# A four-layer scan and attention kernel: three layer scans as one unrolled stream, with layers 1 and 2 at 18 and 36 steps behind layer 0

## The chip, the cores and the metric

The kernel runs on one core of a Trainium2 chip. The time is device microseconds (us) of one execution. TensorE is the matrix engine, VectorE, ScalarE and GpSimd do the elementwise work, and SyncE issues most of the transfers. The profile calls them PE (PEld for its weight loads), DVE, ACT, POOL and SP; a "q" behind a name is that engine's instruction queue.

## The reference, cut to what matters

`x` has shape (batch 8, time 512, features 512), all in fp32. Three recurrent layers run over time, each with a residual, and then one causal attention layer with 16 heads.

```
# layer 0, a gated cell
fused  = sigmoid([x_t, h] @ w_W + w_b)               # (8, 1024)
reset, keep = split(fused, 2)
memory = x_t @ wx_W + wx_b + reset * (h @ wh_W + wh_b)
h      = keep * h + (1 - keep) * tanh(memory)
x = x + all h
# layers 1 and 2, each
h = tanh(x_t @ Wx + b + h @ Wh);   x = x + all h
# layer 3
x = x + attention(x)
```

Step t of a layer needs its own step t-1 and the x of step t that the layer before has left. The products with x_t don't depend on h, so they can be made for many steps at a time.

## The kernel before, in words

**Layout.** All of x stays on chip, transposed, in the tile `X` (feature on 128 partitions, 4 feature groups, batch 8, time 512), so 16 steps of it are (batch, time) with time innermost. `setup` (L398) loads 32 tiles of 128 rows through four buffers `xrows`, turns each with four TensorE transposes (L470) into one of two banks and copies it to `X`, the even ones on VectorE (L508) and the odd ones on ScalarE (L438). ScalarE's queue issues the loads of layer 0's weights, recurrent and input parts by turns. Then GpSimd copies the first 16 steps of `X` into `stage` (L453), and TensorE makes layer 0's 12 groups of products for them (L480).

**Fills.** Time is cut into 32 chunks of 16 steps, so a chunk is 128 columns (16 steps x 8 batches). A *fill* is one group of 128 output features of x @ Wx for one chunk: 16 matmuls in four groups of columns (L225), which VectorE adds a bias to and keeps in `xw0` or `xw12` (L290). Layer 0 has 12 fills a chunk, layers 1 and 2 have 4 each. The matmuls read a chunk from `stage[layer]`, where it lies as (time, batch), contiguous. GpSimd copies it there out of `X` (L381), after VectorE has added the states of the layer before to `X` (L309).

**Steps.** Step n of the stream does on TensorE, in this order: layer 0's products with its state, first those for reset and memory (L181), then those for keep (L187); one product for layers 1 and 2 together (L201); the fills planned for this step (L225). VectorE does in step n: for layers 1 and 2 of step n-1 a transpose out of the bank (L269) and an addition of the input part (L272); it keeps the fills of step n-1 (L290); it does the chunk additions planned here (L309); and then comes layer 0's chain: transpose (L328), addition (L330), transpose and addition for keep (L335, L337), L342 and L345 for the memory, L348, and after ScalarE's tanh L351 and L356, which writes the new state. ScalarE does the tanh of layers 1 and 2 of step n-1 (L237), two sigmoids (L250, L253) and a tanh (L256).

**Rounds and blocks.** A round m is 16 steps; `plan(m)` (L62) says what it holds. Layer 0 runs in rounds 0 to 31 on chunk m, layer 1 in rounds 2 to 33 on chunk m-2, layer 2 in rounds 4 to 35 on chunk m-4, so they are 32 and 64 steps behind. A round's fills are spread evenly over its steps. Four rounds are a block with instruction streams of its own: blocks 0, 4, 28 and 32 are written out, and the five between are a hardware loop over one block. After each block all engines meet and the semaphores are cleared (`clear_signals`, L89), with 9 blocks in all. The last block also loads the attention's weights (L168). A small block adds layer 2's last chunk to `X` on GpSimd (L394). Then come the attention's setup and the attention, which the change leaves alone.

**What sets the order.** Every engine runs its instructions in the written order and waits on counting semaphores.

Of the kernel before, what the change touches and what calls it, by code (L numbers as in the profile page):

```python
# [31 lines left out]
ROUNDS = NCH + 4  # L32
# [3 lines left out]
PER_BLOCK = 4  # L36
RAMP = 8
# [12 lines left out]
def fills_of(m):  # L50

    out = []
    if -1 <= m < NCH - 1:
        out += [(0, g) for g in range(G0)]
    if 0 <= m - 1 < NCH:
        out += [(1, g) for g in range(KC)]
    if 0 <= m - 3 < NCH:
        out += [(2, g) for g in range(KC)]
    return out

def plan(m):  # L62

    fills = fills_of(m)
    n = len(fills)

    late = 0 if m < NCH - 1 else 3
    by_step = [[]] * late + [fills[n * s // (CH - late):n * (s + 1) // (CH - late)] for s in range(CH - late)]
    chunk_ops = [[] for _ in range(CH)]  # L70
    if m < NCH - 1:
        chunk_ops[0].append(("stage", 0, m + 1))
    at = 1
    for layer, c in ((1, m - 1), (2, m - 3)):
        if 0 <= c < NCH:
            chunk_ops[at].append(("add", layer - 1, c))
            chunk_ops[at + 1].append(("stage", layer, c))
        at += 2
    if 0 <= m - 5 < NCH:
        chunk_ops[at].append(("add", 2, m - 5))  # L80
    layers = [l for l, c in ((0, m - 2), (1, m - 4)) if 0 <= c < NCH]
    return {"scan0": 0 <= m < NCH, "scan12": layers, "fills": by_step, "chunk_ops": chunk_ops}
# [17 lines left out]
def scan_rounds(nc, mem, sems, a, first, times):  # L100

    plans = [plan(first + u) for u in range(PER_BLOCK)]
    steps = [(u, t) for u in range(PER_BLOCK) for t in range(CH)]
    S = len(steps)
    if times > 1:
        with nc.Fori(0, times) as i:
            scan_block(nc, mem, sems, a, plans, steps, S, first, i)
            clear_signals(nc, mem)
    else:
        scan_block(nc, mem, sems, a, plans, steps, S, first, None)  # L110
        clear_signals(nc, mem)

def scan_block(nc, mem, sems, a, plans, steps, S, first, i):
    s = sems
    X, stage, h0, h12, xw0, xw12 = mem.X, mem.stage, mem.h0, mem.h12, mem.xw0, mem.xw12

    def counts(per_step):  # L120
        out = [0]
        for u, t in steps:
            out.append(out[-1] + per_step(u, t))
        return out

    n0 = counts(lambda u, t: int(plans[u]["scan0"]))
    n12 = counts(lambda u, t: int(bool(plans[u]["scan12"])))
    nfill = counts(lambda u, t: len(plans[u]["fills"][t]))
    nchunk = counts(lambda u, t: len(plans[u]["chunk_ops"][t]))

    staged = {}

    q = 0
    for u, t in steps:
        for kind, layer, c in plans[u]["chunk_ops"][t]:
            q += 1
            if kind == "stage":
                staged[u, layer] = q
    last_fill = {}
    q = 0  # L140
    for u, t in steps:
        for layer, g in plans[u]["fills"][t]:
            q += 1
            last_fill[u, layer] = q

    def before(u, t):

        return (u % 2, t - 1) if t else (1 - u % 2, CH - 1)

    with nc.Block(no_gpsimd_drain=True) as block:  # L150

        if first == 0:
            @block.sync
            def _(sp):

                for l in (1, 2):
                    for dst, src in ((mem.wx[l], a[f"L{l}_Wx"]), (mem.wh12[:, l - 1, :, :], a[f"L{l}_Wh"])):
                        sp.dma_start(dst[:, :, :], src.rearrange("(k p) n -> p k n", p=P)).then_inc(s.weights_in, 16)
                sp.wait_ge(s.weights_in, 64)

        if first >= NCH:
            @block.sync
            def _(sp):

                loads = [(mem.uk_rows, a["uk_w"]), (mem.uv_rows, a["uv_w"]), (mem.w_proj, a["proj_w"]),
                         (mem.w_qkv, a["qkv_w"])]
                for dst, src in loads:
                    sp.dma_start(dst[:, :, :], src.rearrange("(k p) n -> p k n", p=P)).then_inc(s.weights_in, 16)  # L168
                sp.wait_ge(s.weights_in, 16 * len(loads))

        @block.tensor
        def _(pe):
            def main0(n, u, t):

                if n0[n]:
                    pe.wait_ge(s.h0_new, n0[n])
                us, ts = before(u, t)
                for k in range(KC):
                    for j in range(KC):  # L180
                        mm = pe.matmul(mem.ps0[32 * j:32 * j + B, 0:2 * P],  # L181
                                       h0[:, us, k, ts, :], columns_of(mem.wh0[:, k, 0:3:2, :], j),
                                       start=(k == 0), stop=(k == KC - 1))
                mm.then_inc(s.reset_done, 1)
                for k in range(KC):
                    for j in range(KC):
                        mm = pe.matmul(mem.ps0o[32 * j:32 * j + B, 0:P],  # L187
                                       h0[:, us, k, ts, :], columns_of(mem.wh0[:, k, 1:2, :], j),
                                       start=(k == 0), stop=(k == KC - 1))
                mm.then_inc(s.update_done, 1)  # L190

            def main12(n, u, t):

                if n12[n]:
                    pe.wait_ge(s.h12_new, n12[n])
                us, ts = before(u, t)
                ls = plans[u]["scan12"]
                l0, l1 = ls[0], ls[-1] + 1
                for k in range(KC):
                    for j in range(KC):  # L200
                        mm = pe.matmul(mem.ps12[32 * j:32 * j + B * len(ls), P * l0:P * l1],  # L201
                                       h12[:, us, k, ts, l0:l1, :].rearrange("p l b -> p (l b)"),
# [4 lines left out]
            for n, (u, t) in enumerate(steps):  # L207
                p = plans[u]
                if p["scan0"]:
                    main0(n, u, t)  # L210
                if p["scan12"]:
                    main12(n, u, t)

                if n >= 2 and p["fills"][t] and nfill[n - 1]:
                    pe.wait_ge(s.fill_kept, nfill[n - 1])
                for f, (layer, g) in enumerate(p["fills"][t]):
                    pe.wait_ge(s.chunk_op, staged[u, layer])
                    if first == 0 and layer:
                        pe.wait_ge(s.weights_in, 64)  # L220
                    w = mem.wx[layer]
                    for k in range(KC):
                        for j in range(KC):
                            at = g * P + 32 * j
                            mm = pe.matmul(mem.fillps[n % 2][32 * j:32 * (j + 1), f * N:(f + 1) * N],  # L225
                                           w[:, k, at:at + 32], stage[layer][:, k, :],
                                           start=(k == 0), stop=(k == KC - 1))
                    mm.then_inc(s.fill_done, 1)

        @block.scalar  # L230
        def _(act):
            def tanh12(n, u, t):
                act.wait_ge(s.pre12, n12[n] + 1)

                ls = plans[u]["scan12"]
                l0, l1 = ls[0], ls[-1] + 1
                nc.scalar.activation(h12[:, u % 2, :, t, l0:l1, :].rearrange("p k l b -> p l k b"), mem.sum12[:, l0:l1, :, :],  # L237
                                     ACT.Tanh).then_inc(s.h12_new, 1)

            for n, (u, t) in enumerate(steps):  # L240
                p = plans[u]
                if n:
                    v, w = steps[n - 1]
                    if plans[v]["scan12"]:
                        tanh12(n - 1, v, w)
                if n and t == 0 and p["scan12"] and nchunk[n]:
                    act.wait_ge(s.chunk_op, nchunk[n])
                if p["scan0"]:
                    act.wait_ge(s.pre0, n0[n] + 1)
                    nc.scalar.activation(mem.gates0[:, 0:KC, :], mem.pre0[:, 0:KC, :],  # L250
                                         ACT.Sigmoid).then_inc(s.gates0, 1)
                    act.wait_ge(s.pre0o, n0[n] + 1)
                    nc.scalar.activation(mem.gates0[:, KC:2 * KC, :], mem.pre0[:, KC:2 * KC, :],  # L253
                                         ACT.Sigmoid).then_inc(s.update0, 1)
                    act.wait_ge(s.memory0, n0[n] + 1)
                    nc.scalar.activation(mem.tanh0[:, :, :], mem.mem0[:, :, :],  # L256
                                         ACT.Tanh).then_inc(s.tanh0, 1)
            u, t = steps[-1]
            if plans[u]["scan12"]:
                tanh12(S - 1, u, t)  # L260

        @block.vector
        def _(dve):
            def pre12(n, u, t):

                ls = plans[u]["scan12"]
# [5 lines left out]
                nc.vector.tensor_tensor(  # L272
                    mem.sum12[:, l0:l1, :, :],
                    mem.tp12[:, 0:2 * apart].rearrange("p (l x) -> p l x", l=2)[:, l0:l1, 0:P]
                    .rearrange("p l (q c) -> p l q c", q=KC)[:, :, :, 0:B],
                    xw12[:, u % 2, l0:l1, :, t, :], ALU.add).then_inc(s.pre12, 1)

            def keep_fills(n, u, t):

# [1002 lines left out]
```

## Time and profile before

| | us |
|---|---|
| median of 3 runs | 4083.1 (4080.97 to 4084.29) |
| the profiled execution | 4085.57 |
| its span, first to last instruction | 4083.9 |
| TensorE busy in it | 3902.9 |
| VectorE busy in it | 2336.8 |

The granted TensorE clock has a mean of 0.983 of full speed. Matmuls overlap each other, so their busy time is more than the distance of their starts; for a sum it is the starts that count. A matmul in fp32 is two records, so a group of 16 matmuls stands as x32.

### The profile page before, as it was taken

Reading aid. Unit: us, or ns where it says so; the run is one execution under the profiler, and the core shown is the slowest. Engines: PE = TensorE matmul, PEld = TensorE weight load, DVE = VectorE, ACT = ScalarE, POOL = GpSimd, SP = SyncE. Lnnn points to the kernel's source line nnn. Section 1 sums busy time; section 2 is a strip of 40 time slices with the busy share of each in tenths; the row PEclk is TensorE's granted clock in tenths of the full one; section 3 lists DMA queues with packets and bytes.
Section 4 is the critical chain, followed back from the end, with each engine's and each line's share of the span. In section 5 each row is a group of like instructions: output and inputs, shape, how many; then the busy total and the mean of one; then the engine's idle time right before and its main releaser. Section 6 shows DMA issues by size and latency. Waiting matters only on the chain. (4 is left out here: it accounts for less than half of the span.)

```text
span 4083.9 us, 170825 instructions
## 1 busy us (share of the span) xinstructions
PE 3902.9 (96%) x77684; PEld 2648.1 (65%) x77684; DVE 2336.8 (57%) x8378; ACT 1064.0 (26%) x3931; POOL 158.9 (4%) x373
## 2 busy tenths in 40 slices
PE   6799999999999999999999999998679999999998
PEld 4577777777666666678887777765435555555555
DVE  3565655666566566556556655665326656666564
ACT  1111111111111111111111111111005555555554
POOL 0000000000000000000000000000000000000000
PEclk9999999999999999999999999999969999999999
DMA  5000000000000000000000000001000000000000
GB/s 187 3 4 4 3 3 3 3 4 3 3 3 3 4 3 3 3 4 3 3 4 3 3 3 3 3 3 64 2 6 1 14 11 9 11 12 14 11 6 19
DMA packets 34256, 46.75 MB, mean 11 GB/s; under 512 B 5820, under 2 KB 22252, under 8 KB 33527
## 3 DMA queue, kind: packets, MB, share of 16 engines
q1 hardware_dynamic: 31222, 29.43, 2.3%
q8 instruction: 617, 10.11, 1.0%
q10 hardware_dynamic: 2304, 6.29, 0.4%
q14 instruction: 113, 0.92, 0.1%
HBM read 27.33 MB, written 8.39 MB: 9 GB/s over the span
## 5 line engine op out<-in xcount | busy, mean ns | idle before, releaser
L201 PE MATMUL bank<-wh,h 128*16 128x256 f32 (+1 forms) x17408 | 1002.7, 370 | 52.6 <-ACT h L237 50.8
L181 PE MATMUL bank<-wh,h 128*8 128x256 f32 x16384 | 991.0, 381 | 62.2 <-DVE h L356 31.3
L201 PEld LDWEIGHTS bank<-wh,h 128*16 128x16 f32 (+1 forms) x17408 | 540.1, 97 | 333.9 <-ACT h L237 75.6
L181 PEld LDWEIGHTS bank<-wh,h 128*8 128x8 f32 x16384 | 482.4, 90 | 379.0 <-DVE h L356 50.2
L328 DVE STREAM_TRANSPOSE tp<-bank 128x256 f32<-128x256 f32 x512 | 230.4, 450 | 644.1 <-PE bank L181 644.1
L187 PE MATMUL bank<-wh,h 128*8 128x128 f32 x16384 | 550.9, 274 | 0.0
L187 PEld LDWEIGHTS bank<-wh,h 128*8 128x8 f32 x16384 | 455.6, 90 | 106.2 <-issue 2.5
L250 ACT ACTIVATE gates_sb<-pre_sb 128x32 f32<-128x32 f32 x512 | 117.5, 230 | 1357.6 <-DVE pre_sb L330 1357.6
L225 PE MATMUL bank<-stage,w_qkv 128*32 128x128 f32 x11904 | 386.4, 273 | 0.0
L225 PEld LDWEIGHTS bank<-stage,w_qkv 128*32 128x32 f32 x11904 | 344.3, 110 | 42.6
L237 ACT ACTIVATE h<-sum 128x64 f32<-128x64 f32 (+1 forms) x544 | 137.8, 253 | 786.9 <-DVE sum L272 786.9
L269 DVE STREAM_TRANSPOSE tp<-bank 128x256 f32<-128x256 f32 (+1 forms) x544 | 236.1, 434 | 179.7 <-PE bank L201 118.0
L290 DVE TENSOR_SCALAR xw<-bank,biasT 128x128 f32<-128x128 f32 x628 | 209.6, 349 | 172.3 <-PE bank L225 172.3
L857 ACT ACTIVATE probs<-probs,neg_max 128x385 f32<-128x385 f32 (+3 forms) x512 | 280.2, 554 | 0.0
L870 ACT COPY probsT<-bank 128x512 f32<-128x512 f32 x320 | 174.9, 587 | 369.0 <-PE bank L784 369.0
L946 DVE CUSTOM_DVE_ANT_0 probs<-bank,addends 128x384 f32<-128x384 f32 (+3 forms) x512 | 219.8, 486 | 82.7 <-PE bank L760 80.3
L225 PE MATMUL bank<-stage,wx 128*32 128x128 f32 x8192 | 262.4, 273 | 0.0
L225 PEld LDWEIGHTS bank<-stage,wx 128*32 128x32 f32 x8192 | 235.9, 110 | 29.3
L737 PE MATMUL bank<-X,w_qkv 128*128 128x512 f32 x512 | 236.3, 605 | 9.1 <-PEq L91 5.9
L381 POOL COPY stage<-X 128x512 f32 (+1 forms) x95 | 108.8, 1145 | 2764.6 <-DVE X L309 1387.0
L335 DVE STREAM_TRANSPOSE tp<-bank 128x128 f32<-128x128 f32 x512 | 162.2, 317 | 81.9 <-PE bank L187 77.0
L784 PE MATMUL bank<-ident,probs 128*128 128x128 f32 x1280 | 184.0, 283 | 5.3 <-ACT probs L857 5.0
(131 smaller groups left out, 3346.8 us busy)
## 6 DMA issues: line engine op xcount, KB each, us to landing
xrows<-in_x_dram SPq DMA_DIRECT2D x32, 256.0 KB, 3.8
out_dram<-X SPq DMA_DIRECT2D x32, 256.0 KB, 2.6
w_qkv<-in_L_cond_c_attn_w_dram SPq DMA_DIRECT2D x1, 3072.0 KB, 17.7
wh<-in_L_cond_w_W_dram ACTq DMA_DIRECT2D x4, 512.0 KB, 8.5
w_qkv<-in_L_cond_w_W_dram ACTq DMA_DIRECT2D x4, 512.0 KB, 10.3
wx<-in_L_cond_Wx_dram SPq DMA_DIRECT2D x2, 1024.0 KB, 8.3
wh<-in_L_cond_Wh_dram SPq DMA_DIRECT2D x2, 1024.0 KB, 10.5
mask_all<-in_mask_Bx1x1xS_ff_dram SPq DMA_DIRECT2D x8, 256.0 KB, 3.3
```

Source lines behind the costliest of these rows:

```text
L181: mm = pe.matmul(mem.ps0[32 * j:32 * j + B, 0:2 * P], h0[:, us, k, ts, :], columns_of(mem.wh0[:, k, 0:3:2, :], j), start=(k == 0), stop=(k ...
L187: mm = pe.matmul(mem.ps0o[32 * j:32 * j + B, 0:P], h0[:, us, k, ts, :], columns_of(mem.wh0[:, k, 1:2, :], j), start=(k == 0), stop=(k == K ...
L201: mm = pe.matmul(mem.ps12[32 * j:32 * j + B * len(ls), P * l0:P * l1], h12[:, us, k, ts, l0:l1, :].rearrange("p l b -> p (l b)"), columns_ ...
L225: mm = pe.matmul(mem.fillps[n % 2][32 * j:32 * (j + 1), f * N:(f + 1) * N], w[:, k, at:at + 32], stage[layer][:, k, :], start=(k == 0), st ...
L269: nc.vector.transpose(mem.tp12[:, P * l0:P * l1], mem.ps12[:, P * l0:P * l1]).then_inc(s.turned12, 1)
L290: nc.vector.tensor_scalar(dst, mem.fillps[n % 2][:, f * N:(f + 1) * N].rearrange("p (t b) -> p t b", b=B), mem.biasT[:, bias:bias + 1], No ...
L328: nc.vector.transpose(mem.tp0[:, 0:2 * P], mem.ps0[:, 0:2 * P]).then_inc(s.turned0, 1)
L737: mm = pe.matmul(bank[:, :], mem.w_qkv[:, k, at:at + P], mem.X[:, k, u, :], start=(k == 0), stop=(k == KC - 1))
L784: mm = pe.transpose(bank[:, x * P:(x + 1) * P], mem.probs[qc][:, g, 1 + k * P:1 + (k + 1) * P], mem.ident[:, :])
L857: nc.scalar.activation(row, row, ACT.Exp, bias=mem.neg_max[:, slot, g:g + 1], scale=-1.0, accum_out=mem.sums[:, slot, g:g + 1]).then_inc(s ...
L870: nc.scalar.copy(mem.probsT[v % 2][:, HPG * r * P:HPG * (r + 1) * P], bank[:, :]).then_inc(s.turn_kept, 1)
L946: nc.vector.tensor_tensor_reduce(out=mem.probs[qc][:, g, 1:1 + n], in0=mem.banks[g][:, 0:n], in1=mem.addends[:, TRI[qc]:TRI[qc] + n], scal ...
```

## The change

- All 548 steps (512 of layer 0, and 36 more) are one block, unrolled, with no loop and no meeting of the engines in it. Layer 1 runs 18 steps behind layer 0, layer 2 36 behind.
- Layers 1 and 2 keep their states in a ring of 32 steps. Their places in it and in `xw12` now differ by 2, so VectorE adds the input part for each of the two layers by an instruction of its own.
- The fills have fixed places. In a round of 16 steps, steps 0 and 1 hold two fills of layer 1 each, steps 2 and 3 two of layer 2, and steps 4 to 15 one of layer 0.
- A chunk sum on VectorE (steps 0, 2 and 4) writes x plus the states to `stage`, in (time, batch), for layers 1 and 2; the sum behind layer 2 goes to `X`. A sum whose states wrap around the ring is two instructions. GpSimd has no part in it. `stage` has two slots for each of the two layers.
- Layer 0's fills read the chunk from `X` itself, with batch innermost at a distance of 512 elements.
- Setup loads and turns only 8 of the 32 x tiles (time 0 to 127 of every batch). The other 24 are loaded by SyncE during the scan, turned by TensorE at the end of steps 2 to 25, and copied by ScalarE one step later. The input weights are issued ahead of the recurrent ones. Weights of layers 1 and 2 are loaded between x tiles.
- The weights of the attention are issued when layer 0's last product is done. The last chunk's addition is on VectorE, in the same block.

```diff
-ROUNDS = NCH + 4
-PER_BLOCK = 4
-RAMP = 8
+LAG12 = [CH + 2, 2 * (CH + 2)]
+STEPS = T + LAG12[1]
+HR = 2 * CH
+XR = 4
+TILES = [(b, tc) for tc in range(T // P) for b in range(B)]
+EARLY = B
+TILE_STEP = 2
...
+def fills_of(n):
+
+    m, t = divmod(n, CH)
+    if t < 2 and 0 <= m - 1 < NCH:
+        return [(1, m - 1, 2 * t + g) for g in range(2)]
+    if 2 <= t < 4 and 0 <= m - 2 < NCH:
+        return [(2, m - 2, 2 * (t - 2) + g) for g in range(2)]
+    if t >= 4 and m + 1 < NCH:
+        return [(0, m + 1, t - 4)]
+    return []
+
+
+def sum_of(n):
+
+    m, t = divmod(n, CH)
+    layer = {0: 0, 2: 1, 4: 2}.get(t)
+    if layer is not None and 0 <= m - 1 - layer < NCH:
+        return layer, m - 1 - layer
+    return None
...
+            for i in range(len(tiles)):
+                load_tile(i)
+                if i == XR - 1:
+                    load_layer(1)
+                if i == 2 * XR - 1:
+                    load_layer(2)
...
+                        rows = stage[layer - 1][:, c % 2, k, :] if layer else x_chunk(c)[:, k].rearrange("p b t -> p t b")
...
+            def turn_tile(i):
+                pe.wait_ge(s.x_in[i % XR], 16 * (i // XR + 1))
+                if i >= 2:
+                    pe.wait_ge(s.x_kept, i - 1)
+                for k in range(KC):
+                    mm = pe.transpose(mem.xps[i % 2][:, k * P:(k + 1) * P],
+                                      mem.xrows[:, i % XR, k * P:(k + 1) * P], mem.ident[:, :])
+                mm.then_inc(s.x_turned, 1)
+
+            for n in range(STEPS):
+                if n < T:
+                    main0(n)
+                if layers_of(n):
+                    main12(n)
+                if fills_of(n):
+                    fills(n)
+                if tile_of(n) is not None:
+                    turn_tile(tile_of(n))
...
+            for n in range(STEPS + 1):
+                if n and layers_of(n - 1):
+                    tanh12(n - 1)
+                if n and tile_of(n - 1) is not None:
+                    i = tile_of(n - 1)
+                    b, tc = tiles[i]
+                    act.wait_ge(s.x_turned, i + 1)
+                    nc.scalar.copy(X[:, :, b, tc * P:(tc + 1) * P],
+                                   mem.xps[i % 2][:, :].rearrange("p (k t) -> p k t", k=KC)).then_inc(s.x_kept, 1)
+                if n < T:
+                    gates(n)
...
+                for l in ls:
+                    ins = nc.vector.tensor_tensor(mem.sum12[:, l, :, :], turned[:, l, :, 0:B],
+                                                  xw12[:, l, at[l] // CH % 2, :, at[l] % CH, :], ALU.add)
+                ins.then_inc(s.pre12, 1)
...
+            def chunk_sum(layer, c):
+                if layer:
+                    first = c * CH + LAG12[layer - 1]
+                    dve.wait_ge(s.h12_new, n12[first + CH])
+                    dve.wait_ge(s.chunk_sum, summed[layer - 1, c])
...
+                    if layer < 2:
+                        dst = stage[layer][:, c % 2, :, :].rearrange("p k (t b) -> p k t b", b=B)[:, :, rows, :]
+                        old = before[:, :, rows, :] if layer else in_x.rearrange("p k b t -> p k t b")
+                        ins = nc.vector.tensor_tensor(dst, old, states, ALU.add)
+                    else:
+                        ins = nc.vector.tensor_tensor(in_x, before[:, :, rows, :].rearrange("p k t b -> p k b t"),
+                                                      states.rearrange("p k t b -> p k b t"), ALU.add)
+                ins.then_inc(s.chunk_sum, 1)
...
-            pool.wait_ge(s.x_kept0, len(tiles) // 2)
-            pool.wait_ge(s.x_kept1, len(tiles) // 2)
-            nc.gpsimd.tensor_copy(mem.stage[0][:, :, :].rearrange("p k (t b) -> p k b t", b=B),
-                                  mem.X[:, :, :, 0:CH]).then_inc(s.chunk_op, 1)
...
-            m = 0
-            while m < ROUNDS:
-                times = (NCH - 1 - m) // PER_BLOCK if m == RAMP else 1
-                scan_rounds(nc, mem, sems, a, m, times)
-                m += PER_BLOCK * times
-            add_last_chunk(nc, mem)
+            scan(nc, mem, sems, a)
             clear_signals(nc, mem)
```

## Rows read from the trace of the kernel before

**Rows 1.** The page, part 1: busy us, share of the span and count by engine.

```profile
PE 3902.9 (96%) x77684; PEld 2648.1 (65%) x77684; DVE 2336.8 (57%) x8378; ACT 1064.0 (26%) x3931; POOL 158.9 (4%) x373
```

**Rows 2.** The timeline, all layers: start us, us, engine, line, operation, idle before, releaser.

```profile
1503.07 1.90 PE L181 MATMUL bank<-wh,h 128*8 128x256 f32 x32
1503.32 0.35 DVE L290 TENSOR_SCALAR xw<-bank,biasT 128x128 f32<-128x128 f32 x1 [0.17 <-PE bank L225]
...
1505.05 0.45 DVE L328 STREAM_TRANSPOSE tp<-bank 128x256 f32<-128x256 f32 x1 [1.38 <-PE bank L181]
...
1505.67 1.90 PE L201 MATMUL bank<-wh,h 128*16 128x256 f32 x32
...
1507.32 0.19 DVE L356 TENSOR_TENSOR h<-held,fresh_sb 128x32 f32<-128x32 f32 x1
...
1507.40 1.92 PE L225 MATMUL bank<-stage,wx 128*32 128x128 f32 x64
...
1509.14 1.90 PE L181 MATMUL bank<-wh,h 128*8 128x256 f32 x32
1509.40 0.61 DVE L290 TENSOR_SCALAR xw<-bank,biasT 128x128 f32<-128x128 f32 x2 [1.04 <-PE bank L225]
```

**Rows 3.** The timeline, layer 0 alone: two successive steps.

```profile
75.79 1.91 PE L181 MATMUL bank<-wh,h 128*8 128x256 f32 x32 [0.83 <-DVE h L356]
...
80.28 1.91 PE L181 MATMUL bank<-wh,h 128*8 128x256 f32 x32 [0.83 <-DVE h L356]
```

**Rows 4.** The timeline of TensorE: first instruction of three blocks.

```profile
360.91 1.91 PE L181 MATMUL bank<-wh,h 128*8 128x256 f32 x32 [2.27 <-PEq L91]
...
1064.69 3.60 PE L181 MATMUL bank<-wh,h 128*8 128x256 f32 x32 [5.87 <-issue]
...
2481.33 1.91 PE L181 MATMUL bank<-wh,h 128*8 128x256 f32 x32 [2.08 <-PEq L91]
```

**Rows 5.** The timeline in setup: three turned tiles, the first fills, the scan's first step.

```profile
43.60 2.05 PE L470 MATMUL bank<-ident,xrows 128*128 128x128 f32 x12 [0.39 <-DMA xrows<-in_x_dram]
...
52.67 12.61 PE L480 MATMUL bank<-stage,w_qkv 128*128 128x128 f32 x96 [1.97 <-issue]
...
66.81 1.91 PE L181 MATMUL bank<-wh,h 128*8 128x256 f32 x32 [1.54 <-PEq L91]
```

**Rows 6.** The timeline of the run-out: pairs of successive steps, and the last addition.

```profile
2820.70 1.92 PE L201 MATMUL bank<-wh,h 128*16 128x256 f32 x32 [1.57 <-PEq L91]
2823.73 1.92 PE L201 MATMUL bank<-wh,h 128*16 128x256 f32 x32 [1.11 <-ACT h L237]
...
2920.25 1.06 PE L201 MATMUL bank<-wh,h 128*8 128x128 f32 x32 [1.06 <-ACT h L237]
2922.24 1.06 PE L201 MATMUL bank<-wh,h 128*8 128x128 f32 x32 [0.93 <-ACT h L237]
...
2956.99 1.89 PE L201 MATMUL bank<-wh,h 128*8 128x128 f32 x32 [0.93 <-ACT h L237]
2959.81 1.89 PE L201 MATMUL bank<-wh,h 128*8 128x128 f32 x32 [0.93 <-ACT h L237]
...
2994.78 1.46 POOL L394 TENSOR_TENSOR X<-X,h 128x512 f32<-128x512 f32 x1 [68.77 <-DVEq L389]
```

**Rows 7.** Two stretches: length, busy us (count) by engine, clock, DMA share, GB/s.

```profile
10.00:20.00 10.00, 6.41 (x25) 4.26 (x25) 3.58 (x16) 2.45 (x3) 0.00 (x0) 1.00 1.04 412
...
2953.50:2993.60 40.10, 26.51 (x448) 14.85 (x448) 8.36 (x31) 3.44 (x15) 0.00 (x0) 0.51 0.01 2
```

**Rows 8.** Groups of instructions on VectorE, 300 to 2818: busy, mean ns, idle.

```profile
L272 DVE TENSOR_TENSOR sum<-tp,xw 128x64 f32<-128x64 f32 x447 | 100.7, 225 | 15.4
...
L309 DVE TENSOR_TENSOR X<-X,h 128x512 f32 x60 | 63.3, 1056 | 0.0
...
L272 DVE TENSOR_TENSOR sum<-tp,xw 128x32 f32<-128x32 f32 x13 | 2.5, 193 | 0.4
```

**Rows 9.** The page, part 6: issue of an x tile, KB, us to landing.

```profile
xrows<-in_x_dram SPq DMA_DIRECT2D x32, 256.0 KB, 3.8
```

More of the change, by code:

```diff
@@ L47, with layers_of, counts, ring_parts @@
 NBIAS = _at
[L50 to L58, printed above, removed]
-    return out
[L62 to L82, printed above, removed]
+def layers_of(n):
+    return [l for l in range(2) if 0 <= n - LAG12[l] < T]
+def fills_of(n):
[13 more added lines that the diff above has]
+    return None
+def counts(per_step):
+    out = [0]
+    for n in range(STEPS + 1):
+        out.append(out[-1] + per_step(n))
+    return out
+def ring_parts(first):
+    slot = first % HR
+    head = min(CH, HR - slot)
+    return [(0, slot, head)] + ([(head, 0, CH - head)] if head < CH else [])
 class Mem:
@@ L97, in columns_of @@
     return rows.rearrange("p g (q j r) -> p j g q r", q=KC, j=KC)[:, j]
[L100 to L111, printed above, removed]
@@ L114, in scan_block @@
-def scan_block(nc, mem, sems, a, plans, steps, S, first, i):
-    s = sems
[L116 to L148, printed above, removed]
-    with nc.Block(no_gpsimd_drain=True) as block:
[L152 to L169, printed above, removed]
@@ L171, in _, with main0 @@
         @block.tensor
         def _(pe):
[L173 to L178, printed above, removed]
+            def main0(n):
+                if n:
+                    pe.wait_ge(s.h0_new, n)
+                state = h0_at(n - 1) if n else mem.h0_first
                 for k in range(KC):
@@ new lines, in _ @@
+            for n in range(STEPS + 1):
+                if n and layers_of(n - 1):
+                    pre12(n - 1)
+                if n and fills_of(n - 1):
+                    keep_fills(n - 1)
+                if sum_of(n) is not None:
+                    chunk_sum(*sum_of(n))
+                if n and n < T and n % CH == 0:
+                    dve.wait_ge(s.fill_kept, nfill[n])
+                if n and n % CH == LAG12[0] % CH and n12[n]:
+                    dve.wait_ge(s.fill_kept, nfill[n])
+                if n < T:
+                    step0(n)
@@ L398, in setup @@
 def setup(nc, mem, sems, a):
     s = sems
-    NT = T // P
-    tiles = [(b, tc) for b in range(B) for tc in range(NT)]
+    tiles = TILES[:EARLY]
     loads = []
+    for k in range(KC):
+        rows = slice(k * P, (k + 1) * P)
+        loads.append((mem.wx[0][:, k, 0:2 * D], a["w_W"][rows, :]))
+        loads.append((mem.wx[0][:, k, 2 * D:3 * D], a["wx_W"][rows, :]))
+    FIRST = len(loads)
     for k in range(KC):
@@ L458, in _ @@
             pe.wait_ge(s.ident, 2)
+            for q in range(len(tiles)):
+                pe.wait_ge(s.x_in[q % XR], 16 * (q // XR + 1))
+                if q >= 2:
+                    pe.wait_ge(s.x_kept if q % 2 == 0 else s.x_kept1, q // 2)
+                for k in range(KC):
+                    mm = pe.transpose(mem.xps[q % 2][:, k * P:(k + 1) * P],
+                                      mem.xrows[:, q % XR, k * P:(k + 1) * P], mem.ident[:, :])
+                mm.then_inc(s.x_turned, 1)
             pe.wait_ge(s.small_in, 16 * (1 + len(BIAS_ROWS)))
@@ L667, in attention @@
     s = sems
-    STEPS = UNITS + 3
     order = [(0, *job) for job in HEAD_START]
@@ L823, in _ @@
             pe.wait_ge(s.image_kept, 1)
-            for i in range(STEPS):
+            for i in range(UNITS + 3):
                 if i < UNITS:
@@ L1020, in _ @@
             hidden_extreme(0)
-            for i in range(STEPS):
+            for i in range(UNITS + 3):
                 u, l = i // PER, i % PER
@@ L1107, in __init__ @@
         self.fill_kept = new("fill_kept")
-        self.chunk_op = new("chunk_op")
+        self.chunk_sum = new("chunk_sum")
+        self.layer_in = [new(f"layer{l}_in") for l in (1, 2)]
         self.rows_made = new("rows_made")
```

380 lines of the change are left out of this document (174 added, 206 removed).

## The prediction

> **What bounds the kernel now.** I read the page's busy shares first: TensorE is busy 96% of the span [rows 1], so I asked what it is busy with and whether anything else ends its waits. The timeline of one ordinary stretch of the scan answers that. In a step where layers 0, 1 and 2 all run, TensorE goes from L181 at 1503.07 over L187 to L201, L225 and back to L181 at 1509.14 without a pause, although the new state of layer 0 was there at 1507.32 + 0.19 = 1507.51 [rows 2]. TensorE's own work sets the period. In a step with layer 0 alone it is the other way round: L181 starts 4.49 us apart and has waited 0.83 us for VectorE's state each time [rows 3]. So there are two kinds of step: bound by the loop through VectorE and ScalarE (4.49 us), or bound by TensorE. The same rows price the second kind. L181 and L187 together take 1507.40 - 1503.07 less the 1.73 of L201, 2.60; L201 with both layers 1.73, with one layer half of its 256 columns, 0.87; two fills (two groups of a projection) 1.74, from L225 at 1507.40 to L181 at 1509.14, so one 0.87. Hence all layers with one fill 5.20, with two 6.07, with none 4.33, which the loop makes 4.49; layers 0 and 1 with one fill 4.34 (4.49 by the loop), with two 5.21. Rounds of 16 steps with 20 fills take 12 x 5.20 + 4 x 6.07 = 86.7.
>
> Next, where the span has seams. The starts of blocks of four rounds [rows 4] are 360.91 and, six blocks later, 2481.33: 2120.4 for 24 rounds of 86.7 (2080.8), so 39.6 us lie in six seams. The one at 1064.69 shows of what: 5.87 us of waiting and then 3.60 for L181's 32 records where 1.90 is usual, TensorE at its lower clock. Then the two ends: everything before 66.81 is setup [rows 5], and from 2820.70 to 2993.6 layer 0 is finished and layers 1 and 2 run out [rows 6].
>
> **The change part by part.**
>
> *The order of the scan.* Before, rounds 0 to 31 hold layer 0: rounds 0 to 2 at 16 x 4.49 = 71.8, round 3 (20 fills, layers 0 and 1) 12 x 4.49 + 4 x 5.21 = 74.7, rounds 4 to 30 27 x 86.7 = 2340.9, round 31 (8 fills) 8 x 5.20 + 8 x 4.49 = 77.5; sum 2708.5. The trace has 2820.70 - 66.81 = 2753.9, so seams and small contention are 45.4, in line with 39.6 in six of eight seams. After, the layers start 18 and 36 steps behind instead of 32 and 64. Fills stand two in each of a round's first four steps, one in the other twelve, 20 as before. Rounds 0 and 1: 32 x 4.49 = 143.7 (two fills with layer 0 alone are 4.34, under the loop). Round 2: 4 x 5.21 + 12 x 5.20 = 83.2. Rounds 3 to 30: 28 x 86.7 = 2427.6. Round 31: 4 x 6.07 + 12 x 4.49 = 78.2. Sum 2732.7, **24.2 more** than before, since more of layers 1 and 2 now runs in steps where TensorE is full. The seams go: **-45.4**.
>
> *The run-out.* Before, 64 steps: 32 with both layers 3.04 apart [rows 6], 97.4 in all, then 32 of layer 2 alone, 1.99 apart while the granted clock was 2.4 GHz, and 2.82 apart in the last 14, where the clock of the stretch is 0.51 of full speed, that is 1.2 GHz [rows 7]; 172.9 in all. After, 36 steps. The 18 with both layers get a second VectorE addition on their chain, since the two layers' places in the ring differ by two: the row of the small form costs 193 ns by itself [rows 8], but such instructions overlap, so between 0 and 0.19; I take 0.11. 18 x 3.15 = 56.7, and four of them with two fills need 1.73 + 1.74 = 3.47, +1.3. Of the 18 of layer 2, the first two carry two fills each (2.61) and the first waits for a chunk sum of about 1.06 [rows 8] behind the last tanh: +1.7. If the clock falls after four of them, as it fell before once no fill was left, they take 4 x 1.99 + 1.7 + 14 x 2.82 = 49.1. Sum 107.1, **-65.8**. Bounds: the clock stays up (18 x 1.99 + 1.7 = 37.5, 12 less) or falls in the 14 steps with both layers and no fills (rival below).
>
> *x tiles.* 24 of 32 leave setup. In steps 2 to 25 TensorE turns one each. Twelve transposes took 2.05 with their tail [rows 5], so a tile is 0.6 to 0.68; I take 0.6. Steps 2 to 15 hold 2.60 + 0.87 + 0.6 = 4.07, under 4.49: free. Steps 16 and 17 hold 4.94, steps 20 to 25 also 4.94: 8 x 0.45 = **+3.6** (0 if a transpose overlaps its neighbours, 8 if it doesn't at all). Behind the turn on TensorE's queue stands the next L181, which waits for VectorE anyhow. ScalarE's copy of the tile stands ahead of the next step's sigmoid: it waits for the turn, which ends some 0.4 before the step, takes 0.6 and is done 2 us before the sigmoid's input. SyncE's queue: four tiles and layer 1's weights at once, then one tile per turn, with layer 2's weights between. A tile lands 3.8 us after issue [rows 9], and 2 MB at the 412 GB/s that setup reached [rows 7] are 5 us; the next tile is due two steps or more after its issue, 9 us and up. Free, but a late tile would hold TensorE's queue and with it L181.
>
> *Setup.* Before, tiles came until 50, then the copy on GpSimd, then 12 fills in 12.61 from 52.67, and the scan at 66.81 [rows 5]. After, 2 MB of x and the 3 MB of input weights have to be in first; at 412 GB/s, with 3 us to start, that is 15; the last tiles wait for four buffers and both copies, so I take 21 for the first fill. 12.6 for the fills and the 1.5 of the seam (65.28 to 66.81) give 35.1; I take 36: **-30.8**. The other weights, 3 MB more, are in by 25. Bounds 33 and 42.
>
> *Chunk sums.* Before, three additions a round on VectorE (1.06 each [rows 8]) and three copies on GpSimd. After, three sums a round on VectorE that write the stage directly, and no GpSimd. They stand before L328, which VectorE begins 1.98 after L181 starts. Ahead of the sum at a round's step 0 are one kept fill (ended at 0.60) and the second addition: 0.7 + 1.06 = 1.8, under 1.98. At steps 2 and 4 two kept fills end at 0.87 (L290 at 1509.40 + 0.61 against 1509.14), and half the sums come in two parts: 2.1, so L328 is 0.15 late. That lengthens the loop of 4.49 to 4.64, while these steps are 6.07 and 5.20 long by TensorE: nothing. The rotated read of X is not in the trace. Below, it is the cost of the contiguous form, above, twice 1.06: then L328 is 1.2 late at step 4 against a cover of 0.71, 0.5 x 29 rounds = 14. I take 0, as 1.06 already contains one rotated operand. The fills wait for these sums only 4.33 into the step. The wait for the latest tanh at steps 2 and 4 is covered by the two kept fills, which come 1 us later.
>
> *The fills of layer 0 read X itself*, (time, batch) out of (batch, time), so that successive elements of the moving operand are 2 KB apart. No TensorE row shows such a read. The nearest rows are VectorE's: 64 elements in 225 ns and 32 in 193 give 1.0 ns an element for short runs, and L309, with one operand at steps of 32 B, 1056 ns for 512, about 1.75 ns [rows 8]. So from below nothing, from above 1.75 times: a fill of 1.52 instead of 0.87. I take nothing: the four column groups of a fill each take 128 columns of fp32 in 32 records over 0.87, about 0.85 ns an element and group, much slower than a port need be, but this is the weakest choice here. The Trainium skill ("SBUF — State Buffer", section "Door 1: The DMA port swizzle") says that SBUF has lines of 16 bytes, that full speed needs two hits on a line, and that every crossing to a new line pays a penalty. By that rule each element of these reads pays; it is the second rival.
>
> *The end.* Before, a GpSimd addition of 1.46 in its own block [rows 6], 3.4 us from the last tanh to the next stage. After, a VectorE sum of 1.06 in the same block: **-1.5**.
>
> Sum: +24.2 - 45.4 - 65.8 + 3.6 - 30.8 - 1.5 = **-115.7**. The profiled execution took 4085.6 (span 4083.9), so it would take 3969.9; it lies 2.5 above the median of the runs shown, 4083.1, so on their scale the change gives 3967.
>
> **Rivals.** *The clock falls in the run-out.* With both layers and no fill TensorE works 1.73 of 3.15 (55%); before, five such steps in a row (1.73 of 3.04) kept their speed, and layer 2 alone (0.87 of 1.99) lost it. After there are 14 in a row. At the lower clock each is 1.73 longer: 24, giving 3991. For it speaks the closeness of 55% to 57%, against it that 97 us of such work ran at full clock, with some fills. *The rotated read slows TensorE.* Place: L225's successor for layer 0, 348 of 372 fills in rounds 2 to 30 without cover. Price by L309's ratio 0.65 each, 226, with 8 in setup and some 6 in rounds 0 and 1: 3967 + 240 = 4207, slower. It decides from (4083 - 3967) / 360 = 0.32 us a fill, 1.37 times the time now. For it speaks L309, against it that TensorE asks for an element so seldom. *A late tile or an unrolled stream that starves.* If each tile stalled TensorE by 2 us, 48 us: 4015. Against it: blocks before 710 and after 2481 are unrolled and run at 86.7 a round like the loop.
>
> **How the numbers follow.** The forecast has 0.68, the clock 0.11, the rotated read 0.17, late tiles or starving 0.04. The range is from 3945 (clock up 12, tiles free 4, setup 3 earlier, 3 of small terms) to 4010 (clock 24, sums 14, less those that exclude each other) and leaves out mainly the rotated read. Two runs differ by up to 0.1%, so 0.2% is about what can be told from no change. Faster 0.81; same 0.02, for a read that costs about 0.3 a fill; slower 0.17.
>
> **What would show it.** The first L181 near 36 us; steps of 5.20 and 6.07 with 86.7 a round and no seams from there to about 2775; a fill of layer 0 as long as one of layers 1 and 2 (0.87); both-layer steps of 3.15 at full clock; GpSimd idle; the attention as long as before. A fill above 1.2 us would make the prediction wrong, as would L181 waiting for a tile.

## The result and the profile after

| kernel | median of 4 runs, us | lowest and highest | profiled span, us |
|---|---|---|---|
| before | 4082.03 | 4079.95, 4084.29 | 4083.9 |
| changed | 4327.94 | 4324.08, 4330.54 | 4328.4 |

The ratio is 1.06, with a 95% interval of 1.0583 to 1.0616. The change makes the kernel 246 us slower; the forecast was 116 us faster, so the two lie 362 us apart. The predicted range, 3945 to 4010, does not hold the result.

The changed kernel's page says first that TensorE works more with fewer instructions: part 1 answers to [rows 1] (busy us, share and count by engine).

```profile
PE 4232.9 (98%) x77236; PEld 3661.9 (85%) x77236; DVE 2358.7 (54%) x8864; ACT 1072.4 (25%) x3929; POOL 47.6 (1%) x276
```

448 matmul records went and 330 us of busy time came. Part 5 of the same page (group, count, busy us, mean ns of one, idle time before) says which group it is in.

```profile
L208 PE MATMUL bank<-X,w_qkv 128*32 128x128 f32 x11904 | 797.8, 403 | 0.0
...
L208 PE MATMUL bank<-stage,wx 128*32 128x128 f32 x8192 | 265.7, 273 | 0.7 <-issue 0.7
```

L208 is a fill (L225 before). Both rows have the same weights' shape and the same 128 columns of fp32. One differs from the other in where its columns come from: X, rotated, or the stage, contiguous. A record takes 403 ns against 273. Pipelined records overlap, so the price of a fill has to be read from starts. This is the changed kernel's timeline in one step of all layers, with one fill of layer 0.

```profile
1531.68 2.10 PE L208 MATMUL bank<-X,w_qkv 128*32 128x128 f32 x32
...
1533.44 2.08 PE L167 MATMUL bank<-wh,h 128*8 128x256 f32 x32
...
1537.79 2.11 PE L208 MATMUL bank<-X,w_qkv 128*32 128x128 f32 x32
```

From the fill to the next L167 it is 1533.44 - 1531.68 = 1.76 us, where a fill from the stage takes 0.87 [rows 2]. The step is 1537.79 - 1531.68 = 6.11, not 5.20. Nothing waits inside it, and the stretch from 1500 to 1600 has the full granted clock:

```profile
1500.00:1600.00 100.00, 100.00 (x2247) 100.00 (x2241) 55.55 (x225) 15.58 (x66) 0.00 (x0) 1.00 0.01 3
```

The columns are the stretch, its length, then PE, PEld, DVE, ACT and POOL with counts, and last the clock, DMA share and GB/s. In the same kernel two fills from the stage keep their old price: L208 at 1507.27, here by its 62 records in one piece, to the next step's L167 at 1509.01.

```profile
1507.27 1.97 PE L208 MATMUL bank<-stage,wx 128*32 128x128 f32 x62
1509.01 0.38 PE L167 MATMUL bank<-wh,h 128*8 128x256 f32 x1
```

Setup shows it too. These are the 12 first fills, which now read X and take 21.43 against 12.61 before [rows 5] (1.7 times; the 12.61 are more than their reads alone, see e4), and the scan's first step.

```profile
22.59 21.43 PE L452 MATMUL bank<-X,w_qkv 128*128 128x128 f32 x96 [0.69 <-DVE condT L473]
...
45.58 1.70 PE L167 MATMUL bank<-wh,condT 128*8 128x256 f32 x28 [1.56 <-PEq L100]
```

### The profile page after: what moved, and what is told of

It is laid out like the page before. It is cut to its first block and busy times, and to the rows that moved or that the text cites. A ratio compares the mean times of both kernels' runs of the same rounds, so it can differ in the third digit from the quotient of the medians.

```text
span 4328.4 us, 169650 instructions
## 1 busy us (share of the span) xinstructions
PE 4232.9 (98%) x77236; PEld 3661.9 (85%) x77236; DVE 2358.7 (54%) x8864; ACT 1072.4 (25%) x3929; POOL 47.6 (1%) x276
## 5 line engine op out<-in xcount | busy, mean ns | idle before, releaser
L189 PE MATMUL bank<-wh,h 128*16 128x256 f32 (+1 forms) x16960 | 1065.0, 376 | 33.7 <-ACT h L238 32.4
L167 PE MATMUL bank<-wh,h 128*8 128x256 f32 x16352 | 1052.9, 380 | 6.1 <-DVE h L354 6.1
L167 PEld LDWEIGHTS bank<-wh,h 128*8 128x8 f32 x16352 | 855.1, 93 | 40.2 <-DVE h L354 12.9
L189 PEld LDWEIGHTS bank<-wh,h 128*16 128x16 f32 (+1 forms) x16960 | 808.6, 97 | 70.0 <-ACT h L238 46.9
L208 PE MATMUL bank<-X,w_qkv 128*32 128x128 f32 x11904 | 797.8, 403 | 0.0
L208 PEld LDWEIGHTS bank<-X,w_qkv 128*32 128x32 f32 x11904 | 680.8, 123 | 8.3 <-issue 3.9
L173 PE MATMUL bank<-wh,h 128*8 128x128 f32 x16352 | 610.9, 273 | 0.0
L173 PEld LDWEIGHTS bank<-wh,h 128*8 128x8 f32 x16352 | 568.0, 89 | 8.0
L292 DVE TENSOR_SCALAR xw<-bank,biasT 128x128 f32<-128x128 f32 x628 | 208.7, 349 | 489.4 <-PE bank L208 489.4
L208 PE MATMUL bank<-stage,wx 128*32 128x128 f32 x8192 | 265.7, 273 | 0.7 <-issue 0.7
L208 PEld LDWEIGHTS bank<-stage,wx 128*32 128x32 f32 x8192 | 256.7, 109 | 1.6 <-issue 1.1
L754 PEld LDWEIGHTS bank<-ident,probs 128*128 128x128 f32 x1280 | 138.2, 142 | 75.0 <-issue 45.4
```

The lines of the kernel that those rows point to most:

```text
L167: mm = pe.matmul(mem.ps0[32 * j:32 * j + B, 0:2 * P], state[:, k, :], columns_of(mem.wh0[:, k, 0:3:2, :], j), start=(k == 0), stop=(k == K ...
L173: mm = pe.matmul(mem.ps0o[32 * j:32 * j + B, 0:P], state[:, k, :], columns_of(mem.wh0[:, k, 1:2, :], j), start=(k == 0), stop=(k == KC - 1))
L292: ins = nc.vector.tensor_scalar(dst, mem.fillps[n % 2][:, f * N:(f + 1) * N].rearrange("p (t b) -> p t b", b=B), mem.biasT[:, bias:bias + ...
L754: mm = pe.transpose(bank[:, x * P:(x + 1) * P], mem.probs[qc][:, g, 1 + k * P:1 + (k + 1) * P], mem.ident[:, :])
```

## The experiments

Theory: TensorE itself reads the rotated columns slowly. Rivals: its reads collide with VectorE or ScalarE on the same tensor, or the loss lies in the unrolled stream or the new lags.

### e1: the new order, with the fills reading X in its own order

```diff
-rows = ... x_chunk(c)[:, k].rearrange("p b t -> p t b")
+rows = ... x_chunk(c)[:, k]
...
+made = made.rearrange("p (b t) -> p t b", b=B)   # layer 0 only, in VectorE's keep
```

The same in setup. The fill leaves (batch, time) in PSUM, and VectorE's bias addition reads it rotated.

> The changed kernel, but layer 0's fills read X in its own order (batch, time), runs of 16 neighbouring elements, and VectorE rotates to (time, batch) when it keeps the fill. Theory (the rotated read of the moving operand halves TensorE's rate in layer 0's fills and is the whole loss): a fill takes 0.87 again instead of 1.76, steps with all layers and one fill 5.20 instead of 6.10, setup's 12 fills 12.6 instead of 21.4, and the time is 3970 (3955 to 3990). Rival A (the loss sits in the unrolled stream, the x tiles or the chunk sums): about 4328 or at least above 4200. Rival B (any read that jumps now and then is slow, also in runs of 16): a fill between 0.95 and 1.3, 4000 to 4150.

Measured: 3966.7 us (3966.38 to 3969.08, 4 runs) against 4084.94 for before, ratio 0.972 (0.9702 to 0.9737). Its part 5 and its timeline of one step:

```profile
L208 PE MATMUL bank<-X,w_qkv 128*32 128x128 f32 x11904 | 393.1, 273 | 0.0
...
L294 DVE TENSOR_SCALAR xw<-bank,biasT 128x128 f32<-128x128 f32 x628 | 208.4, 349 | 155.2 <-PE bank L208 121.8
```

```profile
302.67 1.06 PE L208 MATMUL bank<-X,w_qkv 128*32 128x128 f32 x32
303.54 1.91 PE L167 MATMUL bank<-wh,h 128*8 128x256 f32 x32
...
307.87 1.06 PE L208 MATMUL bank<-X,w_qkv 128*32 128x128 f32 x32
```

The fill takes 0.87 and the step 5.20. VectorE pays nothing for reading PSUM rotated: its keeps (L292 in the changed kernel, L294 here) average 349 ns in both. One view of one operand holds the whole loss.

### e2: the fills read a copy that ScalarE has rotated

```diff
+nc.scalar.copy(stage0 as (t b), x_chunk(c).rearrange("p k b t -> p k t b"))   # step 3 of a round
...
-rows = ... x_chunk(c)[:, k].rearrange("p b t -> p t b")
+rows = ... mem.stage0[:, k, :]
```

Setup's 12 fills still read X rotated.

> The changed kernel, but ScalarE copies each chunk of X (one copy in step 3 of a round) to a stage in (time, batch) order and layer 0's fills read that; setup's fills still read X rotated. Theory: fills of layer 0 take 0.87, and only setup keeps 8.8 us of the loss, so 3979 (3965 to 4000). The copy of 512 elements takes 0.6 to 1.1 us on ScalarE and is hidden. Rival (ScalarE's copy holds the sigmoid or the tanh of layers 1 and 2 back): 0.5 to 1 us at each of 31 rounds more, 3995 to 4010. Rival A (the loss is elsewhere): above 4200.

Measured: 3979.89 (3977.57 to 3982.34), ratio 0.9753 (0.9735 to 0.9771).

```profile
L208 PE MATMUL bank<-stage,w_qkv 128*32 128x128 f32 x10720 | 354.0, 273 | 0.0
```

```profile
L266 ACT COPY stage<-X 128x512 f32<-128x512 f32 x27 | 29.8, 1104 | 0.0
```

The same elements in the same order, from a contiguous place, cost 273 ns a record. ScalarE's rotating copy, 1104 ns once a round, delays nothing. The rounds are as long as e1's (71.89, 76.35, 83.28, 86.69). Of the 13.2 us above e1, 8.3 are the setup that is still rotated (scan from 45.66 instead of 37.32), and 3.9 lie in the run-out (from 2784.01 to the next stage at 2895.54, against 2775.67 to 2883.33), where the clock fell sooner.

### e3 and e5: the kernel before, written out, with and without rotated reads

e5 only sets `RAMP = 99`, so that every block of four rounds is written out and none is a pass of the hardware loop. e3 adds the rotated read:

```diff
-stage[layer][:, k, :],
+stage[layer][:, k, :] if layer else chunk[:, k].rearrange("p b t -> p t b"),
```

> The kernel before with all nine blocks written out (no loop) and one thing more: L225's fills of layer 0 read X rotated, as the change does. It still makes the copies to the stage. Against the kernel with the blocks written out alone (sent with it). Theory: 0.90 more for each of 12 fills in rounds 3 to 30, 302, and in rounds 0 to 2, where fills run beside VectorE's and ScalarE's chain, about 0.8 each, 29: some 4058 + 330 = 4390 (4350 to 4440). Rival (the slow fill of the changed kernel comes from its stream or its tiles): the same as the kernel with the blocks written out, within 10 us.

> The kernel before with the five loop passes written out as blocks of their own (RAMP = 99); seams and lags stay. Theory: the seams between loop passes shrink from about 7.5 each to the 2.5 of a seam between written blocks; TensorE keeps its clock there: 4058 (4050 to 4066). Rival (a seam is a seam, however it is written): 4082.

Measured: e5 4057.91 (4055.06 to 4062.11), ratio 0.9941 (0.9921 to 0.9961). e3 4403.78 (4397.63 to 4410.02), ratio 1.0784 (1.0762 to 1.0806). e3 in a stretch of all layers, groups and then two fills in one step:

```profile
L227 PE MATMUL bank<-X,w_qkv 128*32 128x128 f32 x8168 | 570.2, 410 | 0.0
...
L227 PE MATMUL bank<-stage,wx 128*32 128x128 f32 x5376 | 202.8, 273 | 0.0
```

```profile
1506.95 3.89 PE L227 MATMUL bank<-X,w_qkv 128*32 128x128 f32 x64
1510.50 2.08 PE L181 MATMUL bank<-wh,h 128*8 128x256 f32 x32
```

The old order suffers as the new one does: two fills 3.55 instead of 1.74, and 345.9 us between e3 and e5. Order, lags and direct chunk sums are cleared.

e5 prices the hardware loop at 24 to 27 us (4057.91 against the 4082 to 4085 of before) and shows what a seam between two written-out blocks is:

```profile
1056.80 1.94 PE L225 MATMUL bank<-stage,wx 128*32 128x128 f32 x64
1060.56 1.91 PE L181 MATMUL bank<-wh,h 128*8 128x256 f32 x32 [1.82 <-PEq L91]
```

3.76 less the 1.74 of two fills is 2.0, at full clock, where a pass of the loop showed 5.87 of waiting and a lower clock [rows 4].

### e4: the disputed cost by itself

After e1's scan a block of matmuls runs on X, in fours of column groups as a fill has them, each set with another stride.

```diff
+for q in range(16):
+    pe.matmul(fillps[0][32*(q%4):32*(q%4)+32, 0:N], ident[:, 32*(q%4):32*(q%4)+32], flat[:, 0:N*s:s], ...)
```

> The version with X read in its own order, and after the scan a block that measures reads of the moving operand by themselves (16 matmuls of 128 columns each, in four column groups as in a fill, warm; its results are thrown away). Theory (TensorE takes an fp32 element at full rate only where two neighbours lie in the same 16 bytes, as the Trainium skill's page SBUF — State Buffer has it in the section on the DMA port swizzle): steps of 1 and 2 elements 0.87 us, of 4, 8, 32 and the rotated chunk 1.76, of 3 between; runs of 2 every 8, 4 every 16 and 16 every 512 elements 0.87. The same without column groups: 3.5 and 7.0. Rival (every jump costs, whatever the line): steps of 2 already 1.76, runs of 2 about 1.3. Behind it 32 matmuls contiguous and 32 rotated beside VectorE adding in SBUF, then the same beside ScalarE copying in SBUF. Theory of contention (why fills in the first rounds took 2.6 instead of 1.76): contiguous 1.73 as alone, rotated about 5 instead of 3.5 beside VectorE, ScalarE or both. Rival (the 2.6 has another cause, such as waits for instructions): 3.5 in both.

The timeline (L393, L395, L397, L399, L401, L403: every element, every second, third, fourth, eighth, 32nd; L405 and L407: two columns of eight, four of 16; L411: X rotated; L413, L415, L417, L419 and L421: steps of one, two and four, two of eight, and X rotated with full 128x128 weights; L431 and L433 contiguous and rotated, 32 matmuls each, beside ScalarE):

```profile
2910.92 1.08 PE L393 MATMUL bank<-X,ident 128*32 128x128 f32 x32
2911.82 1.10 PE L395 MATMUL bank<-X,ident 128*32 128x128 f32 x32
2912.74 1.59 PE L397 MATMUL bank<-X,ident 128*32 128x128 f32 x32
2914.13 2.04 PE L399 MATMUL bank<-X,ident 128*32 128x128 f32 x32
2915.97 2.06 PE L401 MATMUL bank<-X,ident 128*32 128x128 f32 x32
2917.83 2.96 PE L403 MATMUL bank<-X,ident 128*32 128x128 f32 x32
2920.57 1.18 PE L405 MATMUL bank<-X,ident 128*32 128x128 f32 x32
2921.57 1.06 PE L407 MATMUL bank<-X,ident 128*32 128x128 f32 x32
...
2923.31 3.09 PE L411 MATMUL bank<-X,ident 128*32 128x128 f32 x32
2926.33 3.84 PE L413 MATMUL bank<-X,ident 128*128 128x128 f32 x32
2930.01 3.79 PE L415 MATMUL bank<-X,ident 128*128 128x128 f32 x32
2933.64 7.41 PE L417 MATMUL bank<-X,ident 128*128 128x128 f32 x32
2940.87 3.88 PE L419 MATMUL bank<-X,ident 128*128 128x128 f32 x32
2944.59 7.20 PE L421 MATMUL bank<-X,ident 128*128 128x128 f32 x32
...
2959.69 1.95 PE L431 MATMUL bank<-X,ident 128*32 128x128 f32 x64 [0.73 <-ACT stage L451]
2961.46 4.62 PE L433 MATMUL bank<-X,ident 128*32 128x128 f32 x64
```

Differences of starts, 16 matmuls each:

| columns read | us | against contiguous |
|---|---|---|
| every element | 0.90 | 1 |
| every second | 0.92 | 1.02 |
| every third | 1.39 | 1.5 |
| every fourth, every eighth | 1.84, 1.86 | 2.05 |
| every 32nd (128 B) | 2.74 | 3.0 |
| two of eight (L405) | 1.00 | 1.1 |
| four of 16; X in its own order | 0.87 | 1 |
| X rotated (2 KB apart), up to the next set | 3.02 | 3.4 |
| 128x128 weights, step 1, 2, 4 | 3.68, 3.63, 7.23 | 1, 1, 2 |
| 128x128 weights, two of eight | 3.72 | 1 |

VectorE, ScalarE and GpSimd are busy for 0.00 us from 2910.92 to 2951, so contention is not needed. Beside VectorE's additions 32 contiguous matmuls took 1.77 and 32 rotated ones 4.62 with their tail, and with ScalarE's copies added to them the same two numbers. The rotated ones had been expected at 5 with contention and at 3.5 without, and neither came. The comparison that decides is with e7's L394, where nothing else runs: its first 4.08 us hold 60 records, and the first 4.00 us of L427, beside VectorE, hold 60 too. An engine at work in SBUF adds nothing.

The cost is TensorE's own, and up to a step of eight it goes by how many columns lie within the same 16 bytes: two are enough for nearly the full rate, one gives half of it. The step of three agrees in size. Of each four of its columns, two lie in the same 16 bytes and two stand alone (if X starts at a multiple of 16 bytes, which I take). If every new 16 bytes take the time of two columns, that is 6 for 4, an estimate of 1.5 times, and 1.5 was measured. The far steps, 128 B and 2 KB, cost more than 2.0 in four column groups; e7 takes them up.

The Trainium skill ("SBUF — State Buffer", section "Door 1: The DMA port swizzle") has lines of 16 bytes and says that full speed needs two hits on a line. By that rule the runs of two and the step of two go free and steps of four pay; the trace agrees, and gives the price, 2.0 times. The same section of the Trainium skill also says that one can stride for free up to 4 fp32. There the trace differs: a step of three cost 1.5 times and a step of four 2.0.

### e7: why the probe shows 3.4 and the scan 2.0

e4 left 3.02 for a rotated set where the scan's fill takes 1.76. e7 repeats the probe with longer runs, with fewer column groups, and behind matmuls of 256 columns as in the scan.

> A second measuring block behind the scan (results thrown away). In the first one a rotated read took 1.96 times a contiguous one without column groups, but 3.0 us for 16 matmuls in four groups against 0.87, more than the 1.76 of a fill in the scan, and a run of 32 took 4.62, so it was faster later. Rival (the rate hangs on which part of X is read, not on the order): 64 on the same part take 12, and 16 that go through the four feature groups, as a fill does, take 1.76 wherever they stand.

```profile
2910.83 8.70 PE L394 MATMUL bank<-X,ident 128*32 128x128 f32 x128
2919.13 3.67 PE L396 MATMUL bank<-X,ident 128*32 128x128 f32 x32
2922.64 6.97 PE L398 MATMUL bank<-X,ident 128*32 128x128 f32 x31
...
2944.56 8.14 PE L414 MATMUL bank<-X,ident 128*32 128x128 f32 x127
2952.36 11.45 PE L416 MATMUL bank<-X,ident 128*32 128x128 f32 x128
```

64 rotated matmuls in four column groups (L394) take 8.30, 2.08 per 16. The rival had 12 for them. In one group 16 contiguous ones take 3.51 and 16 rotated ones some 7.0, their records starting 0.22 apart against 0.11 (L396, L398): 2 times, as with full weights. In two groups the records of each also start some 0.22 apart (L402), 2 times, at the lower end of what was expected. 64 with a step of 32 elements (L416) stay at some 2.8 per 16, 3.1 times. Behind matmuls of 256 columns 16 rotated ones took 2.2 and 2.4.

Part of e4's 3.02 comes from what stands behind it. L411 is followed by matmuls on the full 128x128 weights, and the 3.02 runs up to the first of them. Where more rotated matmuls follow, the 17th starts 2.27 after the first (L394) and 2.26 in e4's L427, about 2.5 times a contiguous set. So half the rate is what remains when one column group reads alone, and also in most fills of the scan. With four groups the loss runs from 2.0 to some 3 times, by the stride and by what ran before; what decides in between stays open.

### e6: e1 with TensorE kept busy in the run-out

```diff
+if n >= T + LAG12[0] + 2:
+    for q in range(4):
+        pe.matmul(mem.banks[3][:, 0:P], mem.ident[:, :], mem.ident[:, :], start=True, stop=True)
```

> The version with X read in its own order, and in the 16 last steps (layer 2 alone, no fills) four more matmuls on the identity behind each product, into an unused bank. Theory (those steps are 2.82 instead of 1.99 apart only because the granted clock falls to 1.2 GHz; another 0.9 us of work a step keeps it): 14 x 0.83 = 11.6 less, and the next stage's first matmuls faster too: 3950 to 3956 against 3966.7. Rival (the four matmuls delay the next product, or the clock falls anyway): 3967 to 3975.

Measured in 5 runs: 3961.51 (3960.4 to 3965.05) against 4083.31, ratio 0.97 (0.9686 to 0.9713). This is the best version: 5.2 under e1, though the two were measured in different sets, 3966.7 / 4084.94 = 0.9711 against 3961.51 / 4083.31 = 0.9702, intervals overlapping. The clocks do tell them apart: the mean granted clock is 0.993 to 0.994 in the five runs of e6 and 0.989 to 0.990 in the four of e1. So do the traces. First e1, then e6, in the same place, and each one's stretch from 2853 to 2877.5 (columns as above):

```profile
2855.64 1.90 PE L189 MATMUL bank<-wh,h 128*8 128x128 f32 x32 [0.91 <-ACT h L238]
2858.46 1.89 PE L189 MATMUL bank<-wh,h 128*8 128x128 f32 x32 [0.93 <-ACT h L238]
...
2853.00:2877.50 24.50, 16.88 (x288) 9.55 (x288) 4.16 (x17) 1.83 (x8) 0.00 (x0) 0.50 0.01 1
```

```profile
2857.54 1.06 PE L189 MATMUL bank<-wh,h 128*8 128x128 f32 x32
2858.53 1.16 PE L196 MATMUL bank<-ident 128*128 128x128 f32 x8
2859.62 1.06 PE L189 MATMUL bank<-wh,h 128*8 128x128 f32 x32
...
2853.00:2877.50 24.50, 23.31 (x445) 19.41 (x443) 6.74 (x24) 2.75 (x12) 0.00 (x0) 1.00 0.01 2
```

Steps of 2.08 at the full clock stand against steps of 2.82 at half of it. That would be 7.4 for ten steps by 0.74, less 0.5 for the six that were at full clock anyway and now take 0.09 more, so 6.9. The trace has 6.3 of it: the next stage starts at 2878.40 instead of 2883.33, 4.9 earlier, although the scan had started 1.4 later (38.73 against 37.32; its 12 first fills took 13.88 against 12.90, from the same code). Of the profiled gain 2 are left at the end of the span, where e6's attention ran 3.0 longer. The expected 11 to 16 was for more slow steps than e1 had.

## Why the prediction was wrong, point by point

**The step that failed** is the one headed *The fills of layer 0 read X itself*, where I took nothing for the rotated read. It is worth 0.89 to 0.91 us a fill. The rounds show it: 16 steps took 97.61 in a steady round against e1's 86.69, so 10.9 for 12 fills of layer 0. Changed kernel less e1, by their traces:

| stretch | us |
|---|---|
| setup, scan from 45.58 against 37.32 | 8.3 |
| rounds 0 and 1, 86.76 + 92.94 against 71.89 + 76.36 | 31.5 |
| round 2, 94.12 against 83.28 | 10.8 |
| rounds 3 to 30, 28 x 10.92 | 306 |
| run-out, 109.4 against 105.4 | 4.0 |
| attention to the end, 1084.4 against 1081.9 | 2.5 |

The sum is 363 of the 363.2 between the spans.

The reason given was that 0.85 ns an element and group is much slower than a port need be. It compared a rate that TensorE shows with one that no row showed. The full rate of a matmul was taken for slack in its read port, and e4 has no such slack: the read falls to half the rate as soon as each column has 16 bytes to itself.

**The rival "The rotated read slows TensorE"** is what happened, in its place and with its mechanism; it said 4207. Its price from VectorE's 1.75 times, 0.65, was too low: the ratio is 2.0, so 0.89. And it counted 6 us for rounds 0 and 1, where 31.5 came. With a tile of 0.6 behind the fill the cover there is 0.42 a step in round 0 and nothing in six steps of round 1, so by these rows a doubled fill already costs some 15 (an estimate: 12 x 0.47 + 6 x 0.89 + 6 x 0.74). The other 16 came because these fills took longer than in the full steps:

```profile
112.04 2.71 PE L208 MATMUL bank<-X,w_qkv 128*32 128x128 f32 x32
...
114.68 0.66 PE L218 MATMUL bank<-ident,xrows 128*128 128x128 f32 x4
115.27 1.91 PE L167 MATMUL bank<-wh,h 128*8 128x256 f32 x32
```

From 112.04 to 114.68 it is 2.64. The turned tile behind it (L218) is again a matmul on the full array, as behind e4's L411, and in e1 a contiguous fill in front of a tile takes 0.99. But that is not all: behind the last tile the fills fell only step by step from 2.40 to 1.75 (from 195.70 to 228.76), and in e3, which has no tiles, those of rounds 0 to 2 took 1.75 to 2.7. The rest belongs to e7's open spread. The upper bound of the step was too low for the same reason: a ratio of another engine is not a bound.

**The other terms** can be judged in e1, which has all of the change but that read. Its 3966.7 lies on the forecast of 3967, partly because errors cancel.
- Order: rounds of 86.69 from 37.3 to 2775, no seams: as forecast. Steps 2 to 15 stayed at 4.49 with a tile in each; the free turn is right.
- Seams: -45.4 holds as a term. e5 shows how it is made: 24 to 27 come from writing out the blocks, the rest from having one block.
- Tiles: 4.5, forecast 3.6. The eight full steps take 5.05, not 4.94 (`128.30` to `133.35`, below).
- Setup: scan from 37.3, forecast 36.
- Run-out: 105.4, forecast 107.1, but otherwise than told. The both-layer steps are 3.11 (forecast 3.15), the clock held through them, so the clock rival did not occur. It fell after eight steps of layer 2 alone in e1, where four were forecast, and after four in e2 (its run-out is 3.9 longer) and in the changed kernel (4.0 longer); what decides between four and eight stays open. Against that, TensorE stood still among the first steps with two fills, for 1.31 in issue in one of them (before 2788.63 in e1).
- End: 2.3 from the last tanh's end to the next stage, forecast 1.9; the two parts of the last sum take 1.15.
- Attention, forecast as long as before (1086.9): 1084.4 in the changed kernel and 1081.9 in e1, and with the same code there 1080.4 in e2, 1084.9 in e6 and 1086.7 in e5. Profiled executions differ by that much in it without a cause that I looked for, so it is not read as an effect of the change.
- VectorE's rotated chunk sums take 1.08 to 1.13 each, the contiguous ones 0.68, and delay nothing, as I took it.

e1's timeline for the tile term (a step with one fill and one turned tile):

```profile
128.30 1.91 PE L167 MATMUL bank<-wh,h 128*8 128x256 f32 x32 [0.24 <-DVE h L356]
...
131.78 1.06 PE L208 MATMUL bank<-X,w_qkv 128*32 128x128 f32 x32
132.76 0.66 PE L218 MATMUL bank<-ident,xrows 128*128 128x128 f32 x4
133.35 1.91 PE L167 MATMUL bank<-wh,h 128*8 128x256 f32 x32
```

## What to carry to other kernels

When a copy in front of a matmul is removed, ask what order the copy made: here the moved 512 columns cost 1.1 us on an engine with time to spare and saved TensorE 0.9 us on each of 12 fills. Where a moving operand has to be permuted, let the matmul read memory in its own order and rotate on the way out of PSUM. An access form that no row of the bottleneck engine shows needs, going by this case, a price of at least twice in the range, or a chance of its own as large as that of the forecast.

## What the runs showed that I had not expected

- A matmul of fp32 pays 2.0 times for a moving operand with one column to 16 bytes, and next to nothing for two to 16 bytes; in four column groups far strides cost up to some 3 times.
- VectorE reading PSUM at steps of 64 B takes 349 ns for 128 columns, the same as in the contiguous direction.
- A boundary between two written-out blocks costs 2.0 us at full clock, against 7.6 for the boundary between passes of the loop (5.87 of waiting and 3.60 less 1.90 at the lower clock [rows 4]).
- A few matmuls whose result nobody reads hold TensorE's clock up in a stretch that waits for another engine, for 0.09 us a step here.
